# PSUM buffers of six local-attention layers given out by due time instead of in turn

## What is computed

```python
for i in range(6):
    x = attn_layer(shift_tokens(x), Wqkv[i], q_scale[i], k_scale[i], Wo[i]) + x
    x = ffn_layer(shift_tokens(x), ln_g[i], ln_b[i], W1[i], b1[i], W2[i], b2[i]) + x

def attn_layer(x, Wqkv, qs, ksc, Wo):      # 16 heads of 64
    q, k, v = heads(x @ Wqkv)
    q = rotary(l2norm(q) * qs); k = rotary(l2norm(k) * ksc)
    out = local_attention(q, k, v)         # windows of 32, each sees itself and the one before
    return merge(out) @ Wo                 # 1024 -> 128

def ffn_layer(x, g, bln, W1, b1, W2, b2):  # layernorm, gated gelu, 341 wide
    a, gate = split((layernorm(x) * g + bln) @ W1 + b1)
    return a * gelu(gate) @ W2 + b2
```

## Time and profile before

| what | value |
|---|---|
| time, median of 3 runs | 4593.13 us (4592.19 to 4593.53) |
| profiled execution, first to last instruction | 4596.8 us |
| TensorE matmul busy | 4085.1 us, 89% |
| VectorE (DVE) busy | 3862.2 us, 84% |
| GpSimd (POOL) busy | 3640.7 us, 79% |
| ScalarE (ACT) busy | 3501.9 us, 76% |
| mean granted TensorE clock | 0.956 of full speed |

### The profile page before, as it was taken

The page is one execution under the profiler, slowest core; times in us unless marked ns, Lnnn a source line. Parts: engine busy times, 40 slices in busy tenths (PEclk is TensorE's granted clock), DMA queues, the critical chain, the costliest instruction groups (busy, mean ns, idle before and its releaser), DMA issues.

```text
span 4596.8 us, 140828 instructions
## 1 busy us (share of the span) xinstructions
PE 4085.1 (89%) x57664; PEld 3035.9 (66%) x57664; DVE 3862.2 (84%) x6471; ACT 3501.9 (76%) x6378; POOL 3640.7 (79%) x2624
## 2 busy tenths in 40 slices
PE   7987466557885999999999999999999999999997
PEld 5665345445663667776777767776777777777776
DVE  4664999864555989998999989998999989999994
ACT  4664788874543778887888888887888878888885
POOL 1111888863337999998999999998999999999994
PEclk9999788888997999999999999999999999999999
DMA  2000000000000222222222222222222222222222
GB/s 64 2 2 1 1 1 1 1 1 28 2 2 8 53 55 54 64 66 57 56 60 73 54 61 54 64 69 55 57 59 73 54 61 54 64 70 59 55 58 62
DMA packets 120845, 198.83 MB, mean 43 GB/s; under 512 B 66896, under 2 KB 78224, under 8 KB 120080
## 3 DMA queue, kind: packets, MB, share of 16 engines
q1 hardware_dynamic: 120208, 189.82, 16.7%
HBM read 24.12 MB, written 2.10 MB: 6 GB/s over the span
## 4 chain that ended last, share of the span: by engine, by line
PE 61%; DVE 13%; POOL 12%; issue 8%; ACT 5%; DMA 0%; DVEq 0%; POOLq 0%; SPq 0%; ACTq 0%
PE ps L1306 7%; PE ps L1250 7%; PE ps L1251 6%; PE ps L1317 6%; PE ps L1278 4%; PE ps L1297 3%; PE ps L1290 3%; PE ps L1358 3%; PE ps L1298 3%; POOL arena L1585 3%; POOL arena L1590 2%; PE ps L1347 2%; PE ps L1341 2%; PE ps L1259 2%; DVE arena L1512 2%
## 5 line engine op out<-in xcount | busy, mean ns | idle before, releaser
L1585 POOL TENSOR_TENSOR arena<-arena 128x32 f32<-128x32 f32 x192 | 1138.8, 5931 | 72.3 <-DVE arena L1498 72.3
L1590 POOL TENSOR_TENSOR arena<-arena 128x1024 f32<-128x1024 f32 x384 | 907.1, 2362 | 11.0 <-DVE arena L1489 10.9
L208 POOL TENSOR_SCALAR arena<-arena 128x2 f32<-128x2 f32 x256 | 72.5, 283 | 645.6 <-DVE arena L202 634.4
L1376 ACT ACTIVATE arena<-ps 128x1024 f32<-128x1024 f32 x384 | 391.1, 1021 | 198.3 <-PE ps L1251 193.3
L1488 DVE TENSOR_TENSOR arena<-ps,arena 128x1024 f32<-128x1024 f32 x384 | 468.5, 1220 | 79.6 <-ACT arena L1376 73.3
L1608 POOL TENSOR_TENSOR arena<-arena 128x1536 f32<-128x1536 f32 x192 | 529.0, 2755 | 1.8 <-DVE arena L1522 1.8
L1489 DVE TENSOR_TENSOR arena<-ps,arena 128x1024 f32<-128x1024 f32 x384 | 466.5, 1215 | 0.0
L1306 PEld LDWEIGHTS ps<-arena 96*64 96x64 f32 x12288 | 385.4, 138 | 115.5 <-issue 115.3
L1496 DVE TENSOR_REDUCE arena<-arena 128x32 f32<-128x2048 f32 x192 | 437.0, 2276 | 0.0
L1250 PE MATMUL ps<-arena 128*128 128x512 f32 x768 | 414.5, 622 | 18.4 <-DVE arena L1514 15.8
L1397 ACT ACTIVATE arena<-arena 128x96 f32<-128x96 f32 x1536 | 427.1, 368 | 2.4 <-DVE arena L1514 2.4
(11 more groups left out here) (252 smaller groups left out, 9793.2 us busy)
## 6 DMA issues: line engine op xcount, KB each, us to landing
arena<-arena SPq DMA_DIRECT2D x192, 384.0 KB, 4.3
arena<-arena SPq DMA_DIRECT2D x192, 256.0 KB, 3.7
arena<-arena SPq DMA_DIRECT2D x192, 128.0 KB, 2.3
arena<-in_dWqkv SPq DMA_DIRECT2D x18, 512.0 KB, 3.6
arena<-arena SPq DMA_DIRECT2D x96, 64.0 KB
arena<-arena SPq DMA_DIRECT2D x96, 63.5 KB
arena<-in_dWo SPq DMA_DIRECT2D x6, 512.0 KB, 5.8
arena<-in_x SPq DMA_DIRECT2D x4, 512.0 KB, 7.4
```

Source lines behind the costliest of these rows:

```text
L1585: pool.tensor_tensor(ss[:, 0:32], ss[:, 32:64], mhalf32, ALU.pow).then_inc(*S.rs.up())
L1590: pool.tensor_tensor(a1[:, half], a1[:, half], T2[:, half], ALU.add).then_inc(*radd[g].up())
```

## The change

The class `Slots` takes the place of `Banks` in `phase_d`. A claim gets the buffer whose present holder has the earliest planned time of its freeing piece, and waits for that holder's reader. `frees` names the freeing piece of each kind. All planned times, the list `order`, and so the instructions of every engine in their places, stay as they are; what changes is which buffer a piece has and which earlier piece its claim waits for. The other phases keep `Banks`.

```diff
+class Slots:
+    def __init__(self, n):
+        self.last, self.until, self.place, self.prev = [None] * n, [-1e9] * n, {}, {}
+
+    def take(self, use, until):
+        i = self.until.index(min(self.until))
+        self.place[use], self.prev[use] = i, self.last[i]
+        self.last[i], self.until[i] = use, until
+
+    def slot(self, use):
+        return self.place[use]
+
+    def before(self, use):
+        return self.prev[use]
...
-    bufs = Banks(4)
-    for piece, l, k in order:
-        if piece in ("q0", "q1", "t0", "t1", "s0", "s1", "p0", "p1", "v", "o", "wo"):
-            bufs.take((piece, l * NT + k))
-        if piece in ("sh", "ft", "fg", "fa", "fo"):
-            bufs.take((piece, l * NB + k))
     freed = {"sh": S.xs, "q0": S.ro_q, "q1": S.ro_k, "t0": S.qT, "t1": S.kT, "s0": S.sub0, "s1": S.sub1, "p0": S.pT0,
              "p1": S.pT1, "v": S.vn, "o": S.oT, "wo": S.xxa, "ft": S.fzT, "fg": S.fge, "fa": S.fgm, "fo": S.xxf}
+    frees = {"sh": "xs", "q0": "ro0", "q1": "ro1", "t0": "qT", "t1": "kT", "s0": "mx0", "s1": "mx1", "p0": "pT0",
+             "p1": "pT1", "v": "vn", "o": "oT", "wo": "xxa", "ft": "fzT", "fg": "fge", "fa": "fgm", "fo": "xxf"}
+    bufs = Slots(4)
+    for piece, l, k in order:
+        if piece in frees and piece in TILE:
+            bufs.take((piece, l * NT + k), 1000 * (l * NT + k) + TILE[frees[piece]])
+        if piece in frees and piece in BATCH:
+            bufs.take((piece, l * NB + k), 1000 * (l * NT + 2 * k) + BATCH[frees[piece]])
```

## The result

| kernel | median us | range | runs |
|---|---|---|---|
| before | 4593.33 | 4592.19 to 4596.11 | 4 |
| changed | 4699.47 | 4695.07 to 4704.14 | 4 |

The ratio is 1.023, with a 95% interval of 1.0215 to 1.0244: the changed kernel is 2.3% slower, 106 us. The new class stands ahead of the phase, so its lines are 20 further down: L1250 (q0) is now L1270, L1278 (scores) L1298, L1341 (fg) L1361, L1514 (subtraction) L1534, L1542 (fo's reader) L1562.

What follows compares the result with a forecast made beforehand. TensorE's matmuls were taken to bound the kernel. Stalls of 79 (q0) and 22 (fg), -2 (fa), +2 (phase ends) and 5 (weight loads) made 106 us on 4593.1, so about 4700 us, range 4672 to 4724.

Steps and rivals of the forecast that it cites:

- The pace: TensorE, busy 31.55 of 31.70 us per cycle, sets the pace, so whatever keeps it waiting is paid in full.
- not slower: Rival, chance 0.03: POOL is the true pace and hides TensorE's stall of 1.16 us per cycle; time stays at 4593.
- q0 behind fo: In the half with fo, q0 takes fo's buffer and waits for DVE's L1542: 0.91 us mostly, 79 us together.
- DVE would not catch up: DVE's chain to fo's reader starts at TensorE's scores, 4.3 us against TensorE's 3.6, so the difference returns each cycle.
- One sign: Expected in the changed profile: the chain that ended last goes over DVE twice more in each cycle than before.
- fg behind s1: fg takes s1's buffer, read by DVE's L1514 after fg's start: a stall of 0.25 us 89 times, 22 us.
- q0 in the other half: In the half with fg, q0 keeps s0 as predecessor, so its 11.8 us in 77 waits stay.
- Weight loads: Loads left open behind TensorE's new waits: nothing to 32 us, taken as 0.03 us each, 5 us.
- fa, and the ends: fa's old wait behind q1's reader goes, -2 us; some o and v at the phase's ends wait, +2 us.
- The clock: Rival, chance 0.04: repeated pauses lower TensorE's granted clock, giving 4730 to 4990 us; the forecast expected 0.99 to stay.

Runs made afterwards that it cites:

- e2: Changed kernel with s1's reader counted 10 units later in the rule, so fg takes t1's buffer again and q0 still fo's; 4680.3 us.
- e5: Changed kernel with fo's reader planned at 365 instead of 393, so DVE does it ahead of the sum; q0 keeps fo's buffer; 4627.3 us.
- e1: Changed kernel with fo's reader counted 60 units later in the rule, so q0 takes t0's buffer again and fg still s1's; 4626.2 us.
- e4: Changed kernel with the readers of t0 and t1, both on ACT, counted 160 units earlier in the rule; 4585.5 us, ratio to before 0.9978.
- e6: Changed kernel with every due time shifted to what the trace of the kernel before shows for that reader and half; 4577.5 us, ratio to before 0.9964.
- e7: Changed kernel with fo's reader counted 60 units later and s1's 10 later, so both claims get their old buffers; 4598.2 us, ratio to before 1.0009.
- e3: Kernel before, buffers in turn, with one wait added: q0 in the half with fo waits also for fo's reader; 4664.9 us, ratio 1.0150.
- e8: Kernel before, buffers in turn, with fo's reader planned at 365 so DVE does it ahead of the sum; 4594.2 us, ratio 0.9994.

## Why the prediction was right

**The pace.** The step "TensorE sets it, so a stall in each cycle is paid in full" held: 79.7 us of stall at one claim became 86 us of time in e2, 9.0 of the 86 being at the other half's q0. POOL was the candidate for the rival "not slower", and TensorE has no new wait for it in the steady cycle. The Trainium skill calls the busy share of weight loads a good metric for how close a kernel is to its roofline, the best that the hardware allows ("Trainium Kernel Development and Optimization", section "Performance Expectations"). Read as a measure of slack, the 73% would have given TensorE room and hidden the stall; measured, the weight loads' share fell to 70% (2075.96 of 2970) and the time rose by all of it. Here the end-to-end chain was the better guide.

**q0 behind fo.** Forecast 0.91 us each, 79 us in all; measured 78.9. The start-to-start times rose by 0.91 (3022.24 to 3023.91 against 3009.35 to 3010.11). That DVE would not catch up was the step on which the size hung, and the changed kernel has the chain with the same lengths. e5 shows its cause from the other side. One sign was named wrongly: the chain that ended last goes over DVE once more in each cycle, for q0, and not twice; fg's delay stands in it as 0.08 us of issue and longer matmuls.

**fg behind s1.** Forecast 0.25 us each and 22 us; measured 22.3, and e1 shows it alone. It is 0.24 us nearly everywhere, but 0.57 us in five halves of the last layer, where an edge piece (L1574) stands ahead of s1's reader; the forecast took that into account for q0 and not for fg. **q0 in the other half** keeps its wait; the trace lists 43 such waits instead of 77 because many fall under a line's threshold, while the usual time from the first matmul of the scores ahead of it to q0's is 1.17 us in both traces.

**Weight loads.** The term was bounded by 0 and 32 us and taken as 5. It is 6.9 us, but all of it at fg (some 0.08 x 89) and none at q0. That I gave both 0.03 was wrong in its parts.

**fa, and the ends.** -2 and +2 were taken; -2.8 is seen for fa, and +1.5 where o follows scores at the end.

**What wasn't in the sum.** Pauses of TensorE without a wait, most of the 8.2 us at the other half's q0, and some 7 us of scattered gains that set them off. That the total came out to 1 us is luck in so far as these two cancel; the two main terms owe nothing to it.

**The clock.** Flat at 0.99 in the steady part, with 83 waits of q0 behind fo's reader, 79 of them with 0.8 to 1.5 us of idle time. The Trainium skill's rule ("TensorE: Matmul & The Clock Gate", section "A second HAM failure mode: psum-queue depth-cycling"), that micro-idles while a kernel cycles through PSUM buffers can make the clock oscillate, did not set in at pauses of this size. Longer single pauses went both ways. In e4 those of 2.12 and 1.54 us were each followed by a halved clock. In the changed kernel three of 1.54 to 1.62 us were not, the first of them at the same matmul as e4's 1.54, and neither was one of 1.84 us in e2. The 3.4 us behind that one, at a clock of 1.00:

```profile
3061.30:3064.70 3.40, 3.40 (x8) 1.57 (x9) 2.07 (x4) 1.85 (x5) 3.40 (x2) 1.00 0.03 5
```

So the length of a pause alone doesn't settle it, and what does is not shown here.

**Why the rule picked badly.** The due times are places in the order of an engine, and no clock. Against the plan, as the trace of the kernel before has it, ACT reads t0 and t1 by 186 to 232 units (3 to 3.7 us) early, DVE reads s0, s1 and fo between 63 early and 38 late. The rule compared 393 with 438 and 485 with 489 across two engines; the true order was the reverse, by 2.5 and 3.2 us. e4 and e6 show that the rule itself is sound here: given times that hold across engines it beats giving out in turn by 0.2% and 0.4%.

## What to carry to other kernels

Before buffers are given out by due time, measure for each kind of holder when its reader really ends against the claim, and use these; a plan that only orders each engine's work ranks readers of two engines wrongly. For any such change, subtract reader end from claim start for old and new predecessor: a claim is hurt where claim start minus reader end falls under the hand-over, 0.15 us at q0 (0.145 to 0.148 in its 83 waits for fo's reader), and on an engine without slack it is then paid in every cycle. To see whether the late engine can catch up, look where its chain starts: DVE's started at the stalled engine's own work, and it never did.

## What the runs showed of the hardware

TensorE now and then pauses for 0.6 to 2.1 us at work that waits for nothing that the profile shows, in the traces with several of them mostly some 270 to 300 us apart or about twice that. In the traces of before, changed, e2 and e4 I found thirteen such pauses of over 0.6 us in the steady part, and each ended 2.2 to 2.6 us after the start of a 16 KB packet of the instruction queue, the last before it. In the changed kernel it is this one, in which the last seven score matmuls come late:

```profile
2772.50 0.74 PE L1298 MATMUL ps<-arena 64*64 64x96 f32 x25
2774.78 0.39 PE L1298 MATMUL ps<-arena 64*64 64x96 f32 x7 [1.54 <-issue]
```

The packet started at 2772.4 and took about 1 us. The places recur as well: e1, e2, e4 and e7 have a pause of 1.53 or 1.54 us at this very matmul, and the traces of before, e3, e5, e6 and e8 have none there. That TensorE runs out of fetched instructions is the likely reading, since it would tie the pauses both to the packets and to places in the program; it is argued from these coincidences, and no run varied the fetch. Nor is it settled why e4's trace has more of it than e6's, whose instructions are the same but for semaphores and addresses. Whether the pauses make e4's scatter of 16 us isn't shown either, as only one of its nine runs was traced.
